# Expert weights from silu instead of exp, and a new order of the side steps

## The chip, the core and the metric

One core of a Trainium2 chip runs the whole kernel. Its engines are TensorE (PE in the profile, its weight loads PEld), VectorE (DVE), ScalarE (ACT), GpSimd (POOL) and SyncE (SP, which issues the DMAs). The metric is the time of one execution on the device, in microseconds; lower is better.

## The reference, cut to what matters

Four sequences of 1024 tokens with 128 features go through four residual blocks: a linear attention (a), a mixture of experts, a windowed softmax attention (b), and the same mixture of experts again. The change is in the routing of the experts:

```python
logits = x @ gate_w.T                                   # 32 experts
probs = jax.nn.softmax(logits.astype(jnp.float32), axis=-1)
top_w, top_idx = jax.lax.top_k(probs, TOP_K)            # the best 8
top_w = top_w / jnp.sum(top_w, axis=-1, keepdims=True)
comb = jnp.sum(jax.nn.one_hot(top_idx, NUM_EXPERTS, dtype=x.dtype) * top_w[..., None], axis=1)
...
y = u * jax.nn.silu(g) @ dw.T                           # for each expert, of every token
acc + y * w_e[:, None]
```

All 32 experts are computed for every token, and `comb` is zero for those that aren't among a token's best eight.

## The kernel before

**Tiling and stages.** A row is one sequence, with 8 tiles of 128 tokens. The unit of the expert work is a stage: half a row (four tiles, 512 tokens), first pass or second. `STREAM` lists the 16 stages in their order as (row, f), f being 0 and 1 for the two halves of the first pass and 2 and 3 for those of the second: stage 0 is (0, 0), stage 1 (0, 1), stage 2 (1, 0), stage 8 (2, 1). A stage has 16 chunks of two experts each. Of a chunk, PE computes gate and up (three products each, since weights and activations are split into a high and a low part; `gate_up`, lines 1519 to 1521), ACT takes the silu of the gate (line 1056), DVE multiplies it by up (`gated`, line 1304), POOL multiplies that by the experts' weights, spread over the partitions (`hidden`, line 872), and PE adds the chunk to the output (`down`, line 1542), three chunks later. Three pairs of PSUM banks hold gate and up, so PE runs at most three chunks ahead of ACT and DVE.

**Attention parts.** Between the stages stand parts of the windowed attention, in which no chunk runs: one of 8 tiles for each of the rows 0 to 2, and two of 4 tiles for row 3. A tile goes from PE (scores) to DVE (maxima), ACT (exp), DVE and POOL (normalising), PE (turning), DVE (copies) and PE (mixing).

**Side steps.** All other work is cut into named steps, such as the norms (x_stats, x_rstd, x_apply, x_turn; m_ and s_ for the other two norms), the linear attention (qkv, expo, elu, attend, kvsum, wterm, wred and the h_ steps), its MLP (attnT, mlp1, mlp2) and the routing. The order is written out by hand. `AHEAD` lists the steps that run before the first stage, together with the first six chunks of stage 0 (early n is gate and up of chunk n on PE, lead n its silu and its gated product). `PLAN` has for each stage or part a table from a slot to steps: in a stage, slot s stands behind chunk s on each engine; an attention part has three slots for each tile and three at its end, so 27 for 8 tiles. `own`, `ahead` and `back` say whether a step belongs to the row of the period, the next or the one before. Every engine walks the same list and does its share of each step, in that order, so a step that waits holds up all that stands behind it on its engine. PE's products of the side steps go through one PSUM bank, `side`, in the order of the list.

**The routing steps.** moe_turn, z_hi and z_lo bring the normalised tokens to the form that the products read; route and r_sum give `logits`, 128 tokens x 4 tiles x 32 experts. `top` (DVE) finds the eight largest of each tile, negates the first into `neg_top` and marks the eight in `replaced`. `weigh` (ACT, line 1012) takes exp(logits - maximum), one operation for each tile, since the bias differs. `comb` (DVE, lines 1286 to 1289) keeps the marked ones, sums them and inverts the sum; `cnorm` (ACT, line 1018) scales by it; `weighT` turns the result on PE (line 1461) and copies it (ACT, line 1025). Then SP (`send_weights`, `spread_quarter`) writes it to DRAM and reads it back, spread over 64 partitions for each expert: the first quarter of a stage in 8 DMAs, the others in two each, one buffer for the even quarters and one for the odd. POOL's `hidden` waits for its quarter. SP issues its DMAs in one order too: in the loop over the stages the loads of the next rows of x (`load_rows`) and quarters 2 and 3 of the stage, and then the weights of the next stage. The weights of stage 2 it sends at the end of row 0's attention part, ahead of the loads of row 2.

**Tables of ACT.** exp, gelu and silu each need a table of their own. The compiler puts a table load ahead of an operation whose function differs from the last of these three; copies, squares, relu and scaled copies need none. exp is used by the attention parts, by expo and by weigh, gelu by mlp1, silu by the chunks.

## Time and profile before

| what | value |
|---|---|
| timed runs | 966.5, 966.74 and 979.81 us; median 966.74 us |
| the profiled execution | 970.32 us, its span 968.5 us |
| mean granted clock of TensorE | 0.966 |
| busy share of the span | PE 92%, DVE 67%, ACT 63%, POOL 69% |

The span runs from the first to the last instruction; the execution's own time has 1.8 us around it. The busy share of PE counts matmuls whose ends are modelled, and it is an average over the whole span. The stages lie, by the start of each stage's first gate product, at 65 us (stage 0), 119.5 (stage 1), 217 (stage 2), 270, 311 and 355 (stages 3 to 5); the first attention part lies from 162 to 217 us, the second from 400 to 447.

### The profile page before, as it was taken

To read this page: it belongs to the slowest core of one execution; us is meant where nothing else is said; L and a number is where in the kernel's file an instruction comes from. 1 tells how busy PE (TensorE), PEld (TensorE's weight loads), DVE (VectorE), ACT (ScalarE), POOL (GpSimd) and SP (SyncE) were. 2 spreads that over 40 slices of the span, in tenths; PEclk is the share of its full clock that TensorE was granted. 3 is DMA by queue.
4 is the path that set the end of the run, shared out by engine and by line. 5 is a ranking of instruction groups with operands and counts; after the bars stand their busy time and mean duration, and the time that the engine had idled before them with its cause. 6 is when DMAs were issued, how large, how long until landed. Compare 5 with 4: busy or idle time off the path is not lost.

```text
span 968.5 us, 16816 instructions
## 1 busy us (share of the span) xinstructions
PE 895.2 (92%) x5456; PEld 623.2 (64%) x5456; DVE 653.0 (67%) x1471; ACT 611.6 (63%) x1876; POOL 663.8 (69%) x617
## 2 busy tenths in 40 slices
PE   2467999898999999999999999999999999999998
PEld 1145666685667666687666666687666667667665
DVE  5898876897768748698648756798635348447522
ACT  4446676993665576795775585896556377486531
POOL 6786888675687759576669768666666545646654
PEclk8559999999899999999999999999999999999999
DMA  6006254016343626240433534340344530713352
GB/s 193 0 1 142 52 128 89 2 46 136 64 123 76 139 60 157 58 121 13 98 92 87 146 83 108 74 129 17 87 106 102 135 68 27 159 38 102 88 133 65
DMA packets 64903, 85.75 MB, mean 89 GB/s; under 512 B 5232, under 2 KB 30768, under 8 KB 64560
## 3 DMA queue, kind: packets, MB, share of 16 engines
q1 hardware_dynamic: 64816, 84.68, 36.4%
q8 instruction: 43, 0.70, 0.3%
q14 instruction: 44, 0.36, 0.1%
HBM read 79.39 MB, written 5.28 MB: 87 GB/s over the span
## 4 chain that ended last, share of the span: by engine, by line
PE 69%; DVE 10%; ACT 7%; POOL 5%; issue 4%; DMA 3%; SPq 1%; DVEq 0%; ACTq 0%; POOLq 0%
PE bank L1542 19%; PE bank L1519 11%; PE bank L1521 10%; PE bank L1520 10%; ACT probs L1081 4%; PE bank L1578 4%; PE bank L1563 3%; PE bank L1592 2%; POOL work L872 2%; DVE probsT L1346 2%; PE bank L1406 1%; DMA spread_w<-comb_dram 1%; DVE w_terms L1188 1%; PE bank L1556 1%; DMA x_buf<-x 1%
## 5 line engine op out<-in xcount | busy, mean ns | idle before, releaser
L872 POOL TENSOR_TENSOR work<-work,spread_w 128x512 f32<-128x512 f32 x256 | 333.8, 1318 | 171.0 <-DVE work L1304 151.7
L1304 DVE TENSOR_TENSOR work<-work,bank 128x512 f32<-128x512 f32 x256 | 172.1, 683 | 185.3 <-PE bank L1521 93.1
L1542 PE MATMUL bank<-work,down_w 128*128 128x512 f32 x512 | 262.7, 598 | 1.9 <-POOL work L872 1.9
L1056 ACT ACTIVATE work<-bank 128x512 f32<-128x512 f32 x256 | 150.3, 596 | 176.5 <-PE bank L1521 171.9
L1519 PE MATMUL bank<-z_hi,gate_hi 128*128 128x512 f32 x256 | 168.0, 656 | 4.9 <-ACT work L1056 2.7
L1081 ACT ACTIVATE probs<-bank,neg_max 128x96 f32<-128x96 f32 x512 | 166.3, 386 | 5.5 <-DVE neg_max L1332 3.9
L880 POOL TENSOR_TENSOR probs<-probs,prob_inv 128x768 f32<-128x768 f32 x64 | 95.1, 1486 | 59.9 <-DVE prob_inv L1340 59.6
L1081 ACT ACTIVATION_READ_ACCUMULATOR probs<-bank,neg_max 128x1 f32 x512 | 127.6, 252 | 0.0
L1542 PEld LDWEIGHTS bank<-work,down_w 128*128 128x128 f32 x512 | 95.3, 189 | 29.6 <-POOL work L872 5.6
L1519 PE MATMUL bank<-z_hi,up_hi 128*128 128x512 f32 x256 | 101.8, 397 | 3.1 <-DVE work L1304 3.1
L1521 PE MATMUL bank<-z_hi,gate_lo 128*128 128x512 f32 x256 | 102.0, 398 | 0.0
L1521 PE MATMUL bank<-z_hi,up_lo 128*128 128x512 f32 x256 | 101.5, 397 | 0.0
L1520 PE MATMUL bank<-z_lo,gate_hi 128*128 128x512 f32 x256 | 101.2, 395 | 0.0
L1520 PE MATMUL bank<-z_lo,up_hi 128*128 128x512 f32 x256 | 100.4, 392 | 0.0
L829 POOL TENSOR_TENSOR kv_terms<-elu,qkv 128x1024 f32<-128x1024 f32 x32 | 81.8, 2562 | 12.5 <-DVE elu L1153 7.2
L1346 DVE COPY probsT<-bank 96x512 f32<-96x512 f32 x128 | 80.2, 666 | 3.6 <-PE bank L1578 3.2
L1332 DVE TENSOR_REDUCE neg_max<-bank 128x4 f32<-128x384 f32 x128 | 64.8, 547 | 20.1 <-PE bank L1563 19.2
L1519 PEld LDWEIGHTS bank<-z_hi,gate_hi 128*128 128x128 f32 x256 | 49.0, 191 | 42.4 <-issue 31.0
L1578 PE MATMUL bank<-ident,probs 128*96 128x128 f32 x512 | 69.8, 278 | 6.8 <-DVE probsT L1346 6.0
L1520 PEld LDWEIGHTS bank<-z_lo,gate_hi 128*128 128x128 f32 x256 | 49.3, 193 | 33.7 <-issue 30.6
L1563 PE MATMUL bank<-keysT,qm 32*128 32x96 f32 x1024 | 69.2, 269 | 0.0
L1563 PEld LDWEIGHTS bank<-keysT,qm 32*128 32x128 f32 x1024 | 66.4, 188 | 0.0
(155 smaller groups left out, 1467.2 us busy)
## 6 DMA issues: line engine op xcount, KB each, us to landing
spread_w<-comb_dram SPq DMA_DIRECT2D x96, 512.0 KB, 6.7
spread_w<-comb_dram SPq DMA_DIRECT2D x128, 128.0 KB, 3.0
vals<-v_dram SPq DMA_DIRECT2D x16, 384.0 KB, 4.0
x_buf<-x SPq DMA_DIRECT2D x8, 256.0 KB, 4.3
v_dram<-v_tok SPq DMA_DIRECT2D x8, 256.0 KB, 6.8
out<-xs SPq DMA_DIRECT2D x8, 256.0 KB, 3.1
spread_w<-wg SPq DMA_DIRECT2D x1, 1024.0 KB, 7.1
spread_w<-wu SPq DMA_DIRECT2D x1, 1024.0 KB, 9.2
```

Of the source, the lines that this page charges most:

```text
L872: pool.tensor_tensor(work[:, n % WORK], work[:, n % WORK], spread_w[:, n // EACH % 2, s % EACH], ALU.mult).then_inc(hid_gated, 1)
L880: pool.tensor_tensor(pr, pr, prob_inv[:, i % 2, part].unsqueeze(2).broadcast_to([P, HALF_BLOCKS, KW]), ALU.mult).then_inc(probs_normed, 1)
L1056: act.activation(work[:, n % WORK], bank[GATE_BANKS[ring_of(row, f, s)]], ACT.Silu).then_inc(silu_ready, 1)
L1081: a = act.activation(probs[:, i % 2, m], bank[hg][:, b * KW:(b + 1) * KW], ACT.Exp, bias=neg_max[:, i % 2, m:m + 1], accum_out=prob_sum[:, ...
L1304: dve.tensor_tensor(work[:, n % WORK], work[:, n % WORK], bank[UP_BANKS[ring_of(row, f, s)]], ALU.mult).then_inc(gated_ready, 1)
L1346: dve.tensor_copy(probsT[:, b], bank[4 + b % 2][0:KW, :]).then_inc(probsT_copied, 1)
L1519: pe.matmul(dst, w_hi[:, cols], h, start=True, stop=False)
L1520: pe.matmul(dst, w_hi[:, cols], l, start=False, stop=False)
L1521: pe.matmul(dst, w_lo[:, cols], h, start=False, stop=True).then_inc(ready, 1)
L1542: pe.matmul(bank[Y_BANK], down_w[:, c], work[:, n % WORK], start=(c == 0), stop=(c == CH - 1)).then_inc(down_done, 1)
L1563: mm = pe.matmul(bank[hg][:, KW * b:KW * (b + 1)], qm[feats, i // T, NB * (i % T) + b].rearrange("p j q -> p (j q)"), keysT[feats, first:f ...
L1578: mm = pe.transpose(bank[4 + b % 2][0:KW, P * hg:P * (hg + 1)], probs[:, i % 2, hg * NB + b], ident[:])
```

## The change

With m the maximum of a tile's logits and y = logit - m - 1, which is -1 or less, let s = silu(y) = y sigmoid(y). Then y - s = y (1 - sigmoid(y)), and s / (y - s) = sigmoid(y) / (1 - sigmoid(y)) = exp(y), which differs from the old value by a factor that the later division by the sum takes out. `top` now also subtracts m + 1 from the logits, in place, and signals only after that; `weigh` is one silu of all four tiles; `comb` gets a subtraction, a reciprocal and a multiplication more.

```diff
             def weigh(row, f):
                 act.wait_ge(top_ready, STAGE_AT[row, f] + 1)
-                for t in range(T):
-                    a = act.activation(expd[:, t], logits[:, t], ACT.Exp, bias=neg_top[:, t:t + 1])
-                a.then_inc(expd_ready, 1)
+                act.activation(expd[:], logits[:], ACT.Silu).then_inc(expd_ready, 1)
...
-                dve.tensor_scalar(neg_top[:], top[:, :, 0], -1.0, None, ALU.mult).then_inc(top_ready, 1)
+                dve.tensor_scalar(neg_top[:], top[:, :, 0], -1.0, -1.0, ALU.mult, ALU.add)
                 for t in range(T):
                     ins = dve.match_replace(replaced[:, t], top[:, t], logits[:, t], NEG)
                 step(ins)
+                dve.tensor_tensor(logits[:], logits[:], neg_top[:].unsqueeze(2).broadcast_to([P, T, NE]),
+                                  ALU.add).then_inc(top_ready, 1)
...
+                step(dve.tensor_tensor(logits[:], logits[:], expd[:], ALU.subtract))
+                step(dve.reciprocal(logits[:], logits[:]))
                 step(dve.scalar_tensor_tensor(out=comb[:], in0=replaced[:], scalar=TAKEN, in1=expd[:],
                                               op0=ALU.is_lt, op1=ALU.mult))
+                step(dve.tensor_tensor(comb[:], comb[:], logits[:], ALU.mult))
                 step(dve.tensor_reduce(top_sum[:], comb[:], AX_X, ALU.add))
```

The second part of the change is a new `PLAN` and a new `AHEAD`: the same steps in other slots, throughout. No step is added or dropped. Shown are the list ahead of the first stage, from its middle on, and the tables that the prediction speaks of; the other tables are as thoroughly changed.

```diff
 AHEAD = (
-    own(("masks", 0), ("x_stats", 0), ("x_rstd", 0), ("x_apply", 0), ("x_turn", 0), ("lam", 0),
-        ("qkv_first", 0), ("qkv_first", 1), ("qkv_first", 2), ("elu_first", 0), ("masks", 1), ("attend", 0),
-        ("x_stats", 1), ("elu_first", 1), ("qkv_first", 3), ("w_hi", 0), ("kvsum", 0), ("elu_first", 2),
...
-        ahead(("qkv_next", 0)) + own(("wred", 4), ("kvsum", 5), ("wterm", 5), ("wred", 5), ("kvsum", 6),
-        ("m_apply", 0), ("moe_turn", 0), ("w_lo", 1), ("z_hi", 0), ("z_lo", 0), ("wterm", 6), ("wred", 6)) +
-        ahead(("qkv_next", 1)) + own(("route", 0), ("r_sum", 0), ("attend", 7), ("early", 0), ("top", 0),
-        ("weigh", 0)) + ahead(("qkv_next", 2)) + own(("kvsum", 7), ("comb", 0), ("wterm", 7), ("masks", 2),
-        ("wred", 7), ("cnorm", 0), ("h_sq1", 1)) + ahead(("qkv_next", 3)) + own(("h_red1", 1), ("h_newton1", 1)) +
-        ahead(("expo", 0), ("elu", 0)) + own(("early", 1), ("early", 2), ("weighT", 0), ("lead", 0), ("lead", 1),
-        ("h_g2", 1)) + ahead(("attend", 0)) + own(("h_sq2", 1), ("early", 3), ("early", 4), ("early", 5)) +
-        ahead(("qscale", 0)) + own(("h_red2", 1), ("lead", 2)) + ahead(("attend", 1), ("kvsum", 0)) +
-        own(("lead", 3), ("lead", 4), ("lead", 5))
+    own(("masks", 0), ("x_stats", 0), ("x_rstd", 0), ("x_apply", 0), ("masks", 1), ("x_stats", 1),
+        ("x_rstd", 1), ("w_hi", 0), ("x_turn", 0), ("lam", 0), ("qkv_first", 0), ("qkv_first", 1), ("qkv_first", 2),
+        ("elu_first", 0), ("qkv_first", 3), ("attend", 0), ("elu_first", 1), ("attend", 1), ("elu_first", 2),
...
+        ahead(("x_apply", 0), ("x_turn", 0)) + own(("m_rstd", 0), ("m_apply", 0), ("attend", 7), ("wterm", 6)) +
+        ahead(("qkv_next", 0), ("qkv_next", 1)) + own(("wred", 6), ("moe_turn", 0), ("z_hi", 0), ("masks", 2),
+        ("z_lo", 0), ("route", 0)) + ahead(("qkv_next", 2)) + own(("kvsum", 7), ("wterm", 7), ("r_sum", 0),
+        ("wred", 7), ("h_sq1", 1), ("w_lo", 1), ("h_g2", 1)) + ahead(("qkv_next", 3), ("expo", 0)) +
+        own(("h_red1", 1), ("h_sq2", 1), ("top", 0), ("weigh", 0), ("h_newton1", 1), ("h_red2", 1), ("comb", 0),
+        ("cnorm", 0), ("h_pow2", 1), ("h_newton2", 1), ("early", 0), ("h_scale", 1)) + ahead(("elu", 0)) +
+        own(("early", 1), ("lead", 0), ("weighT", 0)) + ahead(("attend", 0)) + own(("lead", 1), ("early", 2),
+        ("h_gain", 1), ("h_sum", 1), ("lead", 2), ("lead", 3), ("early", 3)) + ahead(("qscale", 0), ("attend", 1),
+        ("kvsum", 0)) + own(("attnT", 1), ("x_add", 1), ("mlp1", 1)) + ahead(("wterm", 0)) + own(("early", 4),
+        ("mlp2", 1), ("lead", 4), ("lead", 5), ("early", 5), ("m_stats", 1))
 )
     (0, "attn"): {
-        0: ahead(("wred", 4), ("wterm", 5), ("z_hi", 0)),
+        0: ahead(("moe_turn", 0), ("z_hi", 0), ("kvsum", 5), ("wred", 4)),
...
-        11: own(("values", 1)) + ahead(("top", 0), ("weigh", 0)),
-        13: own(("bias", 1)),
-        15: ahead(("comb", 0), ("cnorm", 0)),
-        22: own(("proj", 0)),
-        23: own(("m_stats", 2), ("m_rstd", 2)),
-        25: ahead(("weighT", 0)),
+        8: ahead(("kvsum", 6)) + own(("queries", 1), ("queries_copy", 1)),
+        11: ahead(("route", 0), ("r_sum", 0), ("top", 0), ("weigh", 0)),
+        13: ahead(("wterm", 6)) + own(("values", 1)),
+        18: own(("bias", 0)) + ahead(("comb", 0), ("cnorm", 0)),
+        20: ahead(("weighT", 0)),
+        22: own(("bias", 1), ("proj", 0)),
+        26: ahead(("wred", 6)),
     },
     (1, "first"): {
-        0: back(("m_apply", 2)) + own(("kvsum", 6), ("wterm", 6)),
-        2: back(("proj", 1)) + own(("wred", 6), ("kvsum", 7)),
-        3: own(("wterm", 7)) + back(("moe_turn", 2)) + own(("wred", 7)) + ahead(("x_stats", 0)),
+        0: own(("kvsum", 7)),
+        2: back(("m_stats", 2), ("m_rstd", 2)),
+        3: own(("wterm", 7), ("wred", 7)) + back(("proj", 1)) + own(("h_sq1", 1), ("h_g2", 1)),
+        4: ahead(("x_stats", 0)) + own(("h_red1", 1)) + ahead(("x_rstd", 0)),
...
     (1, "attn"): {
-        0: ahead(("weighT", 0)),
+        2: ahead(("wterm", 7)),
...
     (2, "second"): {
-        15: own(("weighT", 1)),
     (2, "third"): {
+        0: ahead(("kvsum", 3), ("wterm", 3)) + own(("weighT", 1)),
...
     (2, "attn"): {
-        0: ahead(("weighT", 0), ("kvsum", 7)) + own(("bias", 1)),
-        2: ahead(("wterm", 7)) + back(("y_back", 3)),
+        0: ahead(("weighT", 0)),
+        2: back(("y_back", 3)),
```

The steps attnT 1, mlp1 1, mlp2 1 and m_stats 1 of row 0 stood in slots 6 and 7 of stage 0 and are now in `AHEAD`. weighT of the next stage stood in slot 14 of stages 0 and 2 and in slot 13 of stage 6, and now stands in slot 15 of them.

## Rows read from the trace of the kernel before

**Rows 1.** The page's first part: busy us, share of span, instructions.

```profile
PE 895.2 (92%) x5456; PEld 623.2 (64%) x5456; DVE 653.0 (67%) x1471; ACT 611.6 (63%) x1876; POOL 663.8 (69%) x617
```

**Rows 2.** The chain of waits by engine, in shares of the span.

```profile
PE 69%; DVE 10%; ACT 7%; POOL 5%; issue 4%; DMA 3%; SPq 1%; DVEq 0%; ACTq 0%; POOLq 0%
```

**Rows 3.** Timeline of PE, 929.8 to 940 us: start, duration, line, operation, tiles.

```profile
930.96 0.79 PE L1519 MATMUL bank<-z_hi,gate_hi 128*128 128x512 f32 x1
...
933.20 0.79 PE L1519 MATMUL bank<-z_hi,gate_hi 128*128 128x512 f32 x1
```

**Rows 4.** PE's waits, 270 to 400 us: total us, times, longest.

```profile
PE bank L1400 <- ACT zT L922: 0.5, 1, 0.5
```

**Rows 5.** Windows: length, busy us (instructions) by engine, PE clock, DMA share.

```profile
20.00:65.00 45.00, 19.61 (x46) 9.76 (x46) 40.97 (x62) 20.28 (x44) 36.45 (x30) 0.50 0.00 1
...
162.00:217.00 55.00, 51.91 (x629) 40.61 (x628) 46.03 (x112) 51.52 (x278) 36.45 (x33) 0.97 0.16 40
217.00:270.00 53.00, 48.26 (x245) 32.57 (x243) 39.75 (x87) 27.71 (x57) 31.93 (x34) 0.94 0.42 91
400.00:447.00 47.00, 45.06 (x623) 35.55 (x622) 39.12 (x83) 45.91 (x263) 32.70 (x30) 1.00 0.30 76
...
37.10:41.50 4.40, 1.65 (x2) 0.50 (x2) 4.02 (x13) 1.39 (x4) 2.96 (x5) 0.50 0.00 0
```

**Rows 6.** Groups by line, table loads: busy us, mean ns | idle before.

```profile
L1056 ACT ACT_TABLE_LOAD x32 | 41.1, 1283 | 1.3 <-ACT combT L1025 0.6 <-ACT v_tok L1048 0.2
...
L1012 ACT ACT_TABLE_LOAD x15 | 19.2, 1283 | 0.3
```

**Rows 7.** Timeline of ACT, 108 to 113 us.

```profile
111.08 1.28 ACT L1056 ACT_TABLE_LOAD   x1
112.38 0.60 ACT L1056 ACTIVATE work<-bank 128x512 f32<-128x512 f32 x1
```

**Rows 8.** Groups by line, DVE.

```profile
L1304 DVE TENSOR_TENSOR work<-work,bank 128x512 f32<-128x512 f32 x256 | 172.1, 683 | 185.3 <-PE bank L1521 93.1 <-ACT work L1056 87.3 <-issue 2.4
...
L1164 DVE TENSOR_REDUCE kv<-kv_terms 128x64 f32<-128x1024 f32 x32 | 38.9, 1214 | 7.9 <-POOL kv_terms L829 7.6
...
L1286 DVE SCALAR_TENSOR_TENSOR comb<-replaced,expd 128x128 f32<-128x128 f32 x16 | 6.7, 416 | 7.9 <-ACT expd L1012 7.3 <-DVE replaced L1278 0.4
...
L1232 DVE RECIPROCAL newton<-head_ms 128x64 f32<-128x64 f32 x8 | 4.4, 553 | 0.3
```

**Rows 9.** Timeline of DVE, in brackets the wait and what ended it.

```profile
13.90 0.43 DVE L1158 SCALAR_TENSOR_TENSOR elu<-elu,qkv 128x256 f32<-128x256 f32 x1 [2.66 <-ACT elu L950]
...
60.42 2.28 DVE L1176 TENSOR_TENSOR up_lo<-spread_w,up_hi 128x2048 fp32r<-128x2048 f32 x1
...
69.87 0.18 DVE L1289 RECIPROCAL top_inv<-top_sum 128x4 f32<-128x4 f32 x1
...
240.33 0.87 DVE L1139 BATCH_NORM_STATS2 stats<-x_buf 128x6 f32<-128x128 f32 x4 [4.50 <-DMA x_buf<-x]
```

**Rows 10.** Chain of waits, 73 to 95 us: start, us, what.

```profile
75.48 0.45 PE bank L1461 x4
```

**Rows 11.** Timeline of POOL, 40 to 125 us.

```profile
92.81 1.29 POOL L872 TENSOR_TENSOR work<-work,spread_w 128x512 f32<-128x512 f32 x1 [4.53 <-DMA spread_w<-comb_dram]
```

**Rows 12.** PE's waits, 65 to 120 us; last row 217 to 270.

```profile
PE bank L1406 <- ACT zT L922: 1.0, 1, 1.0
PE bank L1400 <- ACT z L931: 0.8, 1, 0.8
PE bank L1435 <- ACT attnT L922: 0.7, 1, 0.7
PE bank L1428 <- DVE attn L1240: 0.5, 1, 0.5
...
PE bank L1519 <- DVE work L1304: 3.1, 1, 3.1
```

**Rows 13.** The fused operation of comb: ns min/median/max, first and last start.

```profile
L1286 DVE SCALAR_TENSOR_TENSOR comb<-replaced,expd x16: 280/293/1015, 69.2 to 913.2; 128x128 f32<-128x128 f32 x16
```

More of the change, by code:

```diff
@@ L96 @@
-        11: ahead(("wred", 1)) + own(("route", 1), ("r_sum", 1), ("top", 1)) + ahead(("x_apply", 1)) +
-            own(("weigh", 1)) + ahead(("kvsum", 2)),
-        12: ahead(("x_turn", 1)) + own(("comb", 1)),
-        13: ahead(("qkv", 4), ("wterm", 2)) + own(("cnorm", 1)),
-        14: ahead(("wred", 2)) + own(("weighT", 1)) + ahead(("kvsum", 3), ("wterm", 3)),
-        15: ahead(("qkv", 5)),
+        0: ahead(("wred", 0)),
+        3: own(("m_rstd", 1), ("m_apply", 1)),
+        4: ahead(("x_stats", 1)),
@@ new lines @@
+        5: ahead(("x_rstd", 1)),
+        8: own(("moe_turn", 1), ("z_hi", 1)) + ahead(("kvsum", 1)) + own(("z_lo", 1)) + ahead(("wterm", 1),
+            ("attend", 2)),
+        9: own(("route", 1), ("r_sum", 1)),
+        10: ahead(("x_apply", 1)) + own(("top", 1)),
+        11: own(("weigh", 1), ("comb", 1)),
+        12: ahead(("x_turn", 1), ("wred", 1)),
+        13: ahead(("qkv", 4), ("kvsum", 2), ("wterm", 2), ("attend", 3)),
+        14: ahead(("wred", 2)) + own(("cnorm", 1)) + ahead(("qkv", 5), ("kvsum", 3), ("wterm", 3)),
@@ L149 @@
+        14: own(("h_scale", 1), ("h_gain", 1)) + back(("cnorm", 2)) + own(("h_sum", 1), ("x_add", 1)) +
+            ahead(("qkv", 3)),
+        15: back(("weighT", 2)),
     },
     (1, "second"): {
-        0: ahead(("kvsum", 0), ("qscale", 0), ("attend", 1)) + own(("attnT", 1)),
-        1: own(("mlp1", 1)),
-        2: own(("mlp2", 1), ("m_stats", 1), ("m_rstd", 1)) + ahead(("wterm", 0)),
-        4: ahead(("wred", 0)) + own(("m_apply", 1)),
-        5: ahead(("kvsum", 1), ("attend", 2)),
-        7: own(("moe_turn", 1), ("z_hi", 1)) + ahead(("wterm", 1)) + own(("z_lo", 1)),
@@ L157 @@
-        8: own(("route", 1)) + ahead(("wred", 1)) + own(("r_sum", 1), ("top", 1)),
-        11: ahead(("attend", 3)) + own(("y_back", 0), ("s_stats", 0), ("weigh", 1), ("s_rstd", 0)) +
-            ahead(("kvsum", 2)) + own(("comb", 1)) + ahead(("wterm", 2)),
-        12: ahead(("wred", 2)),
-        13: own(("cnorm", 1), ("s_apply", 0)),
-        14: own(("weighT", 1)),
-        15: ahead(("kvsum", 3)) + own(("seq_turn", 0)) + ahead(("x_stats", 1)),
+        0: ahead(("expo", 0)) + own(("attnT", 1)),
@@ new lines @@
+        2: ahead(("elu", 0), ("attend", 0)) + own(("mlp1", 1)),
+        3: own(("mlp2", 1), ("m_stats", 1)) + ahead(("kvsum", 0)) + own(("m_rstd", 1)),
+        5: ahead(("qscale", 0)) + own(("y_back", 0), ("s_stats", 0), ("m_apply", 1)),
+        6: ahead(("wterm", 0)) + own(("moe_turn", 1), ("z_hi", 1)) + ahead(("wred", 0), ("attend", 1)),
+        7: ahead(("x_stats", 1)),
+        8: own(("z_lo", 1)) + ahead(("kvsum", 1)),
+        9: own(("route", 1), ("r_sum", 1), ("top", 1), ("weigh", 1), ("comb", 1), ("s_rstd", 0)) +
+            ahead(("x_rstd", 1)),
@@ L189 @@
[L189 to L196 removed]
+        1: ahead(("mlp2", 0), ("m_stats", 0)),
@@ L239 @@
+        8: ahead(("attend", 2)),
+        9: own(("weigh", 1)) + ahead(("x_rstd", 1)) + own(("s_apply", 0)) + ahead(("wred", 0)) +
+            back(("m_stats", 3)),
+        11: ahead(("kvsum", 1)),
+        12: ahead(("wterm", 1)) + own(("seq_turn", 0)),
+        13: ahead(("wred", 1), ("x_apply", 1)) + own(("comb", 1)) + ahead(("kvsum", 2)),
+        14: ahead(("wterm", 2), ("attend", 3), ("wred", 2), ("x_turn", 1)),
+        15: back(("m_rstd", 3)) + own(("keys", 0), ("cnorm", 1)),
     },
@@ L290 @@
+        5: own(("h_pow2", 1), ("h_newton2", 1), ("h_scale", 1)) + back(("m_apply", 2), ("proj", 1)),
+        7: back(("moe_turn", 2)) + own(("h_gain", 1), ("h_sum", 1), ("x_add", 1)),
+        8: back(("z_hi", 2), ("z_lo", 2)),
+        9: back(("route", 2), ("r_sum", 2), ("top", 2)),
+        10: own(("attnT", 1)) + back(("weigh", 2)),
+        11: back(("comb", 2), ("cnorm", 2)),
+        13: back(("weighT", 2)),
     },
```

349 lines of the change are left out of this document (164 added, 185 removed).

## The prediction

> **What bounds the kernel now.** I read the page first: TensorE (PE) is busy 895.2 of 968.5 us [rows 1]. The chain of waits says the same: 69% of the span is PE, 10% VectorE (DVE), 7% ScalarE (ACT) [rows 2]. Since a busy PE can hide small gaps, I then looked at a stretch with no side steps: the first product of a chunk starts at 930.96 and the next chunk's at 933.20, so a chunk takes 2.24 us [rows 3], and 256 chunks need 573 us however the other engines do. From 270 to 400 us, a stretch of three expert stages full of side steps, PE waited for another engine 0.5 us in all [rows 4]. There a cheaper ACT or a dearer DVE step changes nothing. What is left are three places, which the windows show [rows 5]: the lead-in (20 to 65 us: PE 19.61 of 45, DVE 40.97, so DVE bounds, at half clock), the first attention part (162 to 217: PE 51.91, ACT 51.52, DVE 46.03 of 55, all three near full) and the stage after it (217 to 270: PE 48.26 of 53 at a mean clock of 0.94). A later attention part (400 to 447) has PE 45.06, ACT 45.91 and DVE 39.12 of 47. The change is judged by these.
>
> **ACT: what the formula takes away.** Each exp inside an expert stage costs a table load before it, and one before the next silu. The trace has 15 loads at the exp line and 32 at the silu line [rows 6], 1.283 us each. Walking ACT's program order in the source, counting a load at each change of function among exp, gelu and silu, gives 66 loads before (those two lines agree) and 40 after: 26 fewer, 26 x 1.283 = 33.4 us of ACT. Nearly all is hidden: the chain of waits shows ACT's silu loads only twice, once behind a weigh, at 111.08 [rows 7], once behind a gelu, which stays. So on the path it is worth 1.3 us, and I count that below with the stage where it lies. The load at 111.08 is followed by the silu at 112.38, so a switch costs its 1.283 us and nothing more [rows 7]. The Trainium skill (ScalarE: Activation LUTs, "What ACT_TABLE_LOAD costs") adds a drain to every switch and gives about 2.66 us in all; by it ACT would be freed of 26 x 2.66 = 69 us rather than 33, but as an estimate for the path it would still be one switch. The first attention part goes the other way: its weigh is now silu among exps, so it gets two loads, +2.6 us, where ACT has 3.5 us free [rows 5].
>
> **DVE: what it adds.** Per weigh an add, a subtraction and a multiplication of 128x128 and a 128x128 reciprocal. No such reciprocal is in the trace. The step comb's fused operation of the same shape has two operands from SBUF, as the new ones have, and averages 0.416 us [rows 8]. Reciprocals: 0.553 us for 64 columns [rows 8] and 0.18 for 4 [rows 9]; the line through both gives 0.95 us for 128 columns, which I take because both ends are this kernel's; the bounds are 0.553 and twice that, 1.11. Sum 3 x 0.416 + 0.95 = 2.2 us a weigh (1.8 to 2.4), 35 us in all, and weights that come later by that and by the match_replace that top_ready now follows. In the expert stages the cover is DVE's idle time ahead of the gated product, 185.3 us over 256 chunks or 11.6 a stage [rows 8]; if it were gone, 2.2 us a stage would reach PE two chunks later. Uncovered are the weighs of the lead-in and of the first attention part.
>
> **The lead-in and stage 0.** The new order puts x_stats 1 and w_hi 0 into DVE's 2.66 us wait at 13.9 us [rows 9]; I take 2.2 us gained (0 to 2.66). z_lo now follows w_lo 1 at 62.7 [rows 9]; in the new list two steps of the linear attention of about the same length stand there instead, so z_lo comes at 60.5. From there to the end of comb, at 70.05 now [rows 9], the new list has three such steps as before, and besides w_lo 1 (2.28 us) [rows 9], h_red1, h_newton1 and h_red2 of the second half (for the first half the stretch from 37.1 to 41.5, with 4.02 us of DVE) [rows 5] and the new formula (2.2). So comb ends 8.5 - 2.2 = 6.3 us later, at 76.35, and with about 1 us for cnorm the transposition of the weights can run at 77.4. Now it runs at 75.48 [rows 10], since it stood behind a gate product that waited. So the weights leave 1.9 us later. POOL's fifth hidden product, at 92.81 now [rows 11], comes 17.3 us behind that transposition because its quarter of the weights comes last: +1.9. Against it, attnT 1, mlp1 1, mlp2 1 and their waits (0.5 and 0.7 us) leave stage 0 for the time in which POOL waits anyway, and two more PE waits of stage 0 go, 1.0 us for zT behind the weigh's table load and 0.8 us for z [rows 12]: -3.0. Net -1.1 us; bounds -4.8 (the weights not later, half a chunk gained) and +5 (PE, waiting with a lower clock, loses the 1.9 us twice, and none of the waits goes).
>
> **First attention part and the stage after.** Into attention 0 go kvsum 5 and 6, wterm 6 and wred 6, about 1.2 us each [rows 8], 4.8 us; m_stats 2 leaves it, 1.3 us (0.87 for the statistics, as in [rows 9], the rest an estimate for their aggregation); the formula adds 2.2: 5.7 us of DVE. DVE is busy 84% of this part, so I take 84%, +5 us (0 if all falls into its idle time, +8.3 with ACT's two loads on top). After it, the first expert stage of row 1 loses time for one reason that I can see. SP sends the weights of that stage and only then loads the next rows of x; DVE's x_stats waits 4.50 us for them, until 240.33 [rows 9], with the gated products queued behind it, and PE waits 3.1 us for those [rows 12]; the clock of 0.94 over 53 us is another 3.2 us [rows 5]. The new order transposes these weights in slot 20 of 27 instead of 25; at 55/27 us a slot that is 10 us earlier, SP is past them 10 us earlier, and the rows are there in time. I take -6 (0 to -6.3).
>
> **The rest.** Attention 1 gets wterm 7 (+1.2), attention 2 loses kvsum 7 and wterm 7 (-2.4): at 83% busy -1 (-2.4 to +1.2). weighT of stage 8 moves from the last slot of the stage before into slot 0 of its own; 17.3 us from transposition to the fifth product stand against seven chunks of 2.24 us, 15.7, and what side steps lie between them: +1 (0 to +3). Other PE steps only change places in stages where PE has no gap: 0 (-2.6 to +2).
>
> **Sum.** -1.1 + 5 - 6 - 1 + 1 = -2.1 us. The profiled execution took 970.32 us, its span 968.5 and 1.8 around it; it stands 3.6 above the median of the three timed runs, 966.74. So 968.2 in a profiled execution, and 966.7 - 2.1 = **964.6 us** timed.
>
> **Rivals.** (a) *Weights too late*, ending on the slower side: the formula lengthens the path from logits to weights by 2.2 us and more, and four transpositions move to slot 15 or 0. For: POOL's 4.53 us wait at 92.81 [rows 11]. Against: from slot 15 eight chunks, 18 us at least, are left for the 17.3. It decides when a quarter lands after its chunk's down product is due; each such stage then loses about 3.1 us of waiting and 3.2 of clock as in [rows 5, 12]. One such stage and the upper price of attention 0: 964.6 + 6.3 + 3.3 = 974; four stages: 990. (b) *The new order gains more*: the lead-in's idle PE is the only large reserve, 25 us of the 45 [rows 5]. If DVE's list there is 4.8 us better and attention 0 costs nothing, 964.6 - 3.7 - 5 = 956; below 947 it would need 10 us more of that lead-in, for which DVE has only 4 us of idle time in that window. (c) *DVE and POOL block each other*: comb's fused operation takes 0.280 us at best and 1.015 at worst [rows 13], so it sometimes stands still while POOL works. If the three new ones always took 1.015, a weigh costs 1.8 us more: 29 us, of which the lead-in and attention 0 show 3.6, and POOL's products as much: 964.6 + 7 = 972. The Trainium skill (SBUF — State Buffer, "SBUF: two separate sides") has this as a rule: a DVE operation with two SBUF inputs and a GpSimd operation exclude each other for the whole instruction. It speaks against this change, which adds 48 such operations; the mean of 0.416 shows it to strike rarely. (d) *The loads don't vanish*, if the silu of the weigh were given a table of its own: ACT as before, and the order alone remains, 966.
>
> **How the numbers follow.** Forecast 0.54, (a) 0.19 (of it 0.05 four stages late), (b) 0.17 (of it 0.08 below 947), (c) 0.08, (d) 0.02. Two per cent, 19 us, is about what a measurement of this kernel can tell from no change, since the three runs spread by 13 us. So faster 0.08, the same 0.87, slower 0.05. The range of 8 in 10 takes in (c), most of (a) and the nearer half of (b), and the bounds of lead-in and attention 0: 953 to 977.
>
> **What the profile would show.** 40 table loads, none at the weigh line but two, ACT some 40 us less busy, DVE some 35 more. Reciprocals of 0.95 us. The weights' first transposition at 77 and stage 0 ending at 118.4 instead of 119.5. A first attention part of 60 us, DVE over 85% busy in it, and no DVE wait for x in the stage behind. PE without waits in the later expert stages. The prediction is wrong if the lead-in moves by more than 5 us, or if PE waits for POOL in expert stages.

## The result, and the profile after

The changed kernel takes 980.64 us (median of four, 978.22 to 985.28) against 966.91 for the kernel before beside it: a ratio of 1.0124, with a 95% interval of 1.0093 to 1.0155. It is slower, by less than 2%, where I had forecast 2 us faster; the time lies above my range. The profiled execution took 979.21 us, span 977.5, so 8.9 us over that of before. A ratio leaves out executions more than 1.5% above the fastest of their kernel; in run e4 below these are three of ten, the profiled one (978.95 us) among them.

What the change does to the engines came out as worked out. First part of the page after, to be read beside [rows 1]:

```profile
PE 903.9 (92%) x5456; PEld 628.7 (64%) x5456; DVE 686.3 (70%) x1535; ACT 566.2 (58%) x1802; POOL 671.8 (69%) x617
```

Groups by line of the changed kernel: table loads at the silu and at the weigh line, then the formula's new operations (busy us, mean ns), beside [rows 6, 8].

```profile
L1057 ACT ACT_TABLE_LOAD x17 | 21.8, 1283 | 0.3
...
L1014 ACT ACT_TABLE_LOAD x2 | 2.6, 1283 | 0.0
...
L1290 DVE RECIPROCAL logits<-logits 128x128 f32<-128x128 f32 x16 | 15.2, 953 | 0.6
...
L1281 DVE TENSOR_TENSOR logits<-logits,neg_top 128x128 f32<-128x128 f32 x16 | 7.2, 453 | 0.5
L1293 DVE TENSOR_TENSOR comb<-comb,logits 128x128 f32<-128x128 f32 x16 | 5.8, 360 | 0.5
L1289 DVE TENSOR_TENSOR logits<-logits,expd 128x128 f32<-128x128 f32 x16 | 5.6, 347 | 1.9 <-ACT expd L1014 1.9
```

ACT is 45.4 us less busy, of which 33.4 are the 26 loads; DVE 33.3 more. Neither can be read off the total, since PE is busy 903.9 of the 977.5 us. So the time must be looked for by stretch. I took the start of each stage's first gate product (line 1519 before, 1525 after) in both traces; my terms of the sum stand beside the differences:

| stretch | before, us | after, us | difference | forecast |
|---|---|---|---|---|
| lead-in and stage 0 | 119.5 | 118.3 | -1.2 | -1.1 |
| stage 1 with attention 0 | 97.4 | 101.8 | +4.4 | +5 |
| stage 2 | 52.9 | 46.2 | -6.7 | -6 |
| stages 3 and 4 | 85.1 | 84.8 | -0.3 | 0 |
| stage 5 with attention 1 | 89.8 | 100.0 | +10.2 | +1 |
| stages 6 to 9 with attention 2 | 220.9 | 223.1 | +2.2 | -1 |
| rest | 303.0 | 303.3 | +0.3 | 0 |

One row is off by ten. Windows of the changed kernel (busy us, then the granted clock, DMA share, GB/s), beside [rows 5]:

```profile
162.00:220.00 58.00, 52.11 (x629) 40.17 (x628) 50.73 (x119) 53.44 (x273) 38.78 (x36) 0.97 0.17 38
220.00:266.00 46.00, 44.08 (x239) 30.08 (x238) 37.62 (x88) 22.10 (x54) 30.54 (x33) 1.00 0.44 104
400.00:427.00 27.00, 26.13 (x366) 20.69 (x365) 24.64 (x51) 26.30 (x156) 18.29 (x16) 1.00 0.35 92
424.00:434.00 10.00, 8.91 (x91) 7.27 (x91) 7.21 (x16) 6.33 (x38) 7.16 (x7) 0.68 0.57 129
434.00:444.00 10.00, 10.00 (x90) 8.34 (x88) 5.79 (x12) 5.52 (x34) 4.29 (x5) 0.50 0.00 0
```

In the second attention the granted clock is 1.00 (2.4 GHz) until 427 us and then 0.50 (1.2 GHz); the clock's own records put the fall at 427.64, inside PE's wait shown next, and the return 23.9 us later, where the part ends. Before, it was 1.00 throughout [rows 5]. From 434 to 444 PE is busy 10.00 of 10 us: at the low level PE sets the pace alone, and nothing can be caught up. PE's timeline shows what went before (its first row, from the lead-in, is taken up further below):

```profile
76.80 1.04 PE L1467 MATMUL bank<-ident,comb 128*32 128x128 f32 x4 [4.01 <-ACT comb L1019]
...
423.43 1.08 PE L1584 MATMUL bank<-ident,probs 128*96 128x128 f32 x8
...
425.75 1.08 PE L1598 MATMUL bank<-probsT,vals 96*32 96x128 f32 x32
427.92 1.94 PE L1584 MATMUL bank<-ident,probs 128*96 128x128 f32 x8 [1.09 <-POOL probs L883]
```

The same eight turnings take 1.08 us and then 1.94. Between them PE waited 1.09 us for POOL's normalising. POOL's timeline there:

```profile
422.39 1.27 POOL L860 TENSOR_TENSOR x_buf<-x_buf,bout_all 128x512 f32<-128x512 f32 x1
423.62 1.47 POOL L883 TENSOR_TENSOR probs<-probs,prob_inv 128x768 f32<-128x768 f32 x1
425.17 1.27 POOL L842 TENSOR_TENSOR attn<-attn,g_row 128x512 f32<-128x512 f32 x1
426.41 1.46 POOL L883 TENSOR_TENSOR probs<-probs,prob_inv 128x768 f32<-128x768 f32 x1
```

Two side steps of 1.27 us, bias (line 860) and h_g2 (842), stand ahead of two normalisings in a row (883). The new order has bias 1 in slot 11 and h_sq1 1, h_g2 1 in slot 12; the old one had bias and h_sq1 in slot 9 and h_g2 in 13. In the kernel before, two normalisings (at 424.17 and 426.82) lie between the same two steps (lines 857 and 839 there), and from 395 to 450 us PE never waits for POOL:

```profile
422.81 1.27 POOL L857 TENSOR_TENSOR x_buf<-x_buf,bout_all 128x512 f32<-128x512 f32 x1
...
428.25 1.27 POOL L839 TENSOR_TENSOR attn<-attn,g_row 128x512 f32<-128x512 f32 x1
```

### The profile page after: what moved, and what is told of

Same layout as the page of the kernel before. It is cut to its first block and busy times, and to the rows that moved or that the text cites. A ratio compares the mean times of both kernels' runs of the same rounds, so it can differ in the third digit from the quotient of the medians.

```text
span 977.5 us, 16807 instructions
## 1 busy us (share of the span) xinstructions
PE 903.9 (92%) x5456; PEld 628.7 (64%) x5456; DVE 686.3 (70%) x1535; ACT 566.2 (58%) x1802; POOL 671.8 (69%) x617
## 5 line engine op out<-in xcount | busy, mean ns | idle before, releaser
L875 POOL TENSOR_TENSOR work<-work,spread_w 128x512 f32<-128x512 f32 x256 | 340.2, 1345 | 149.4 <-DVE work L1310 135.5
L1082 ACT ACTIVATE probs<-bank,neg_max 128x96 f32<-128x96 f32 x512 | 165.9, 382 | 14.6 <-DVE neg_max L1338 13.3
L1526 PE MATMUL bank<-z_lo,up_hi 128*128 128x512 f32 x256 | 100.2, 392 | 0.0
L1584 PE MATMUL bank<-ident,probs 128*96 128x128 f32 x512 | 75.5, 293 | 9.6 <-DVE probsT L1352 5.8
L1525 PEld LDWEIGHTS bank<-z_hi,gate_hi 128*128 128x128 f32 x256 | 48.9, 191 | 40.9 <-issue 33.3
L1584 PEld LDWEIGHTS bank<-ident,probs 128*96 128x96 f32 x512 | 57.4, 134 | 23.2 <-issue 11.7
L1569 PE MATMUL bank<-keysT,qm 32*128 32x96 f32 x1024 | 71.8, 277 | 0.0
```

The lines of the kernel that those rows point to most:

```text
L875: pool.tensor_tensor(work[:, n % WORK], work[:, n % WORK], spread_w[:, n // EACH % 2, s % EACH], ALU.mult).then_inc(hid_gated, 1)
L1082: a = act.activation(probs[:, i % 2, m], bank[hg][:, b * KW:(b + 1) * KW], ACT.Exp, bias=neg_max[:, i % 2, m:m + 1], accum_out=prob_sum[:, ...
L1525: pe.matmul(dst, w_hi[:, cols], h, start=True, stop=False)
L1526: pe.matmul(dst, w_hi[:, cols], l, start=False, stop=False)
L1569: mm = pe.matmul(bank[hg][:, KW * b:KW * (b + 1)], qm[feats, i // T, NB * (i % T) + b].rearrange("p j q -> p (j q)"), keysT[feats, first:f ...
L1584: mm = pe.transpose(bank[4 + b % 2][0:KW, P * hg:P * (hg + 1)], probs[:, i % 2, hg * NB + b], ident[:])
```

## The experiments

My main theory (A): that crowding makes the wait, the wait brings the lower clock, and that costs the ten microseconds. Rivals: the formula itself (B, later split into its table loads, T, and its DVE work, D), another moved step (C), values that come late in attention 0 (V). Each ratio is against runs of the kernel before on the same chip (their medians 966.91 to 970.28 us). The two columns on the right are the stretches of the table above, from the profiled execution.

| run | median us | ratio (95%) | stage 1 + attention 0 | stage 5 + attention 1 |
|---|---|---|---|---|
| e1_formula | 985.18 | 1.0193 (1.0137 to 1.0249) | 112.7 | 91.7 |
| e2_order | 978.77 | 1.0093 (1.0062 to 1.0123) | 107.0 | 90.4 |
| e3_split | 974.59 | 1.0065 (1.0037 to 1.0092) | 103.1 | 89.2 |
| e4_crowd | 972.65 | 1.0019 (0.9989 to 1.0048) | 96.3 | 100.5 |
| e5_tables | 987.18 | 1.0171 (1.0128 to 1.0213) | 107.8 | 91.8 |
| e6_hybrid | 978.65 | 1.0111 (1.0054 to 1.0168) | 96.5 | 91.6 |
| e7_spread | 977.65 | 1.0077 (1.0052 to 1.0102) | 112.0 | 89.2 |
| e8_mend | 978.61 | 1.0077 (1.0038 to 1.0115) | 103.4 | 89.2 |
| e9_values | 984.48 | 1.0127 (1.0071 to 1.0183) | 108.5 | 89.2 |
| e10_best | 980.74 | 1.0101 (1.0060 to 1.0141) | 110.6 | 91.3 |
| e11_cut | 973.60 | 1.0055 (1.0019 to 1.0090) | 97.4 | 89.7 |
| e12_again | 982.52 | 1.0103 (1.0051 to 1.0155) | 103.9 | 100.0 |
| e13_early | 978.07 | 1.0079 (1.0044 to 1.0115) | 107.4 | 89.2 |
| e14_both | 972.34 | 1.0034 (1.0004 to 1.0063) | 100.2 | 97.6 |
| e16_red | 971.22 | 1.0028 (0.9992 to 1.0063) | 99.8 | 89.3 |
| e15_mix | 970.75 | 1.0012 (0.9974 to 1.0050) | 106.4 | 93.4 |
| e17_turn20 | 963.06 | 0.9952 (0.9921 to 0.9983) | 101.6 | 91.2 |
| e18_turn17 | 963.44 | 0.9955 (0.9933 to 0.9977) | 97.0 | 89.7 |

**The crowd in slots 11 and 12.** e3 moves one step out of it in the changed kernel, e4 puts the crowd into the kernel before, e12 is the changed kernel again.

```diff
 e3, (1, "attn") of the changed kernel
-        12: ahead(("h_sq1", 1), ("h_g2", 1)),
+        12: ahead(("h_sq1", 1)),
+        16: ahead(("h_g2", 1)),
 e4, (1, "attn") of the kernel before
-        9: ahead(("wred", 7)) + own(("bias", 1)) + ahead(("h_sq1", 1)),
-        13: ahead(("h_g2", 1)),
+        9: ahead(("wred", 7)),
+        11: own(("bias", 1)),
+        12: ahead(("h_sq1", 1), ("h_g2", 1)),
```

> The changed kernel with one step moved: the gain of row 1's second half (a POOL multiplication of 1.27 us) goes from slot 12 of the second attention to slot 16. A: TensorE no longer waits 1.09 us for the normalising at 427, the granted clock stays at 1.0 from 400 to 450 us, the second attention's last-chunk gap falls from 58.1 to 47 to 49 us, and the time is 968 to 971 us. B and C: the fall stays, 977 to 983 us.

> The kernel before with three steps put where the changed kernel has them: bias of row 1 in slot 11 of the second attention, square and gain of the next half in slot 12. A: a wait of TensorE for POOL's normalising of 0.8 us or more there, the clock falls to 0.5, and the time rises by 6 to 11 us to 973 to 978 us. If the attention of the kernel before, in which VectorE is late and POOL has time in hand, takes the two POOL steps without a wait, no change (966 to 968 us): then the crowding counts only together with something else of the change. B and C: 966 to 968 us.

> The changed kernel itself once more. Theory A: the fall of the clock near 427 us recurs with the same wait of 1.1 us for POOL, stage and second attention 99 to 101 us together, time 978 to 985 us. If the fall was that one execution's chance: 89 to 91 us in this profile, and times from 968 us on.

Windows of e3 and then of e4, 430 to 452 us, PE's wait in e4, and two of PE's waits in e12, the first of them for later:

```profile
430.00:452.00 22.00, 19.66 (x278) 15.90 (x275) 20.04 (x44) 18.19 (x98) 16.82 (x18) 1.00 0.23 51
```

```profile
430.00:452.00 22.00, 21.91 (x179) 18.11 (x180) 12.37 (x24) 14.32 (x80) 10.59 (x11) 0.50 0.07 19
```

```profile
429.91 1.94 PE L1579 MATMUL bank<-ident,probs 128*96 128x128 f32 x8 [1.14 <-POOL probs L881]
```

```profile
212.85 1.76 PE L1598 MATMUL bank<-probsT,vals 96*32 96x128 f32 x32 [2.66 <-DMA vals<-v_dram]
...
431.83 1.94 PE L1584 MATMUL bank<-ident,probs 128*96 128x128 f32 x8 [1.09 <-POOL probs L883]
```

With h_g2 four slots later the wait and the fall are gone, and the stretch is 89.2 us instead of 100.0; with the crowd the kernel before gets both, and 100.5 instead of 89.8. In e12 all recurs, down to the 23.9 us. A holds in the profiled executions of these runs. In the times it is worth less: e3's ratio is 1.0065 where the changed kernel has 1.0124 and 1.0103, an estimate of 4 to 6 us for the crowd, and e3 missed its 968 to 971 us; it lies 6 us above the kernel before. Of e4's ten executions six took 970 to 973 us, one 962.68 and three 979 to 987; the median, 972.65, is 4 us above the kernel before and just short of the 973 to 978 expected. So, to judge by the times, the crowd doesn't bring the fall each time.

**Formula and order by themselves.** e1 has the old order and the new weights, e2 the new order and the old weights.

> The new weights from silu with the order of steps of the kernel before. Theory A (the three steps bias, square and gain that stand together in slots 11 and 12 of the second attention keep POOL from the normalising; TensorE waits 1.09 us for it, its granted clock falls from 1.0 to 0.5 and stays there for 24 us, which costs about 10 us): this kernel does not have them together, so no fall of the clock between 390 and 460 us, and 963 to 968 us, ratio to the kernel before 0.996 to 1.001. Theory B (the formula costs the time: four more VectorE instructions for each weighing and weights that come later): 972 to 982 us, the second attention longer than 50 us. Theory C (another of the moved steps): as A here.

> The new order of steps with the old weights (four exponentials for each weighing). A: the three steps stand together as in the changed kernel, so the clock falls to 0.5 in the second attention and the time is 975 to 985 us. B: without the formula the loss goes, 958 to 966 us. C: as A in time, 975 to 985 us.

e1 overturned my view that the formula costs nothing: it is the slowest of all, and its loss lies in attention 0, 112.7 against 97.4. In e2 PE waits just as in the changed kernel, yet the clock stays at 1.00 in this execution:

```profile
435.10 1.08 PE L1581 MATMUL bank<-ident,probs 128*96 128x128 f32 x8 [1.10 <-POOL probs L883]
```

So a wait of 1.1 us can come with the fall and need not. What else decides is open. e2's loss in the profile is in attention 0 too, where its clock was low for 17 us from 204; that its time lies in A's range of 975 to 985 us is luck.

**What the formula does in attention 0.** Its weighing of stage 2 lies there. On e1, e5 takes the table loads away and keeps DVE's work; e6 takes both.

```diff
 e5 and e6, weigh
-                act.activation(expd[:], logits[:], ACT.Silu).then_inc(expd_ready, 1)
+                how = ACT.Exp if (row, f) == (1, 0) else ACT.Silu
+                act.activation(expd[:], logits[:], how).then_inc(expd_ready, 1)
 e6, comb
+                formula = (row, f) != (1, 0)
+                if formula:
+                    step(dve.tensor_tensor(logits[:], logits[:], expd[:], ALU.subtract))
+                    step(dve.reciprocal(logits[:], logits[:]))
...
+                if formula:
+                    step(dve.tensor_tensor(comb[:], comb[:], logits[:], ALU.mult))
```

> The old order with the new weights, but the one weighing that lies inside the first attention (row 1, first quarter) applies exp instead of silu, so the table of the attention's own exponentials stays loaded; VectorE's formula for it is still done, its last product into a buffer that nobody reads. Theory T (the formula alone cost 17 us because this weighing puts two table loads, 2 x 1.28 us, between the exponentials of an attention; TensorE waits and its granted clock falls there for up to 27 us): the first attention takes 97 to 101 us with its stage instead of 112.7, time 968 to 974 us. Theory D (VectorE's four more instructions, 2.2 us, are what delays the attention): no change, 982 to 987 us.

> As the run before, and VectorE's three further operations of the formula for that weighing (subtract, reciprocal, product: 1.5 us) are left out too. T: within 2 us of the run before, 967 to 973 us. D: the whole loss goes only here, 967 to 971 us against 982 to 987 us in the run before.

Timeline of DVE in e5, then PE's wait for the copy at its end:

```profile
206.56 0.37 DVE L1287 TENSOR_TENSOR logits<-logits,expd 128x128 f32<-128x128 f32 x1
206.97 0.95 DVE L1288 RECIPROCAL logits<-logits 128x128 f32<-128x128 f32 x1
...
208.93 0.18 DVE L1294 RECIPROCAL top_inv<-top_sum 128x4 f32<-128x4 f32 x1
209.03 0.19 DVE L1345 RECIPROCAL prob_inv<-prob_sum 128x8 f32<-128x8 f32 x1
209.13 1.26 DVE L1351 COPY probsT<-bank 96x512 f32<-96x512 f32 x2
```

```profile
209.94 1.91 PE L1583 MATMUL bank<-ident,probs 128*96 128x128 f32 x8 [1.55 <-DVE probsT L1351]
```

The comb step stands in one piece, 206.56 to 209.1, ahead of the copy of probsT; PE waits 1.55 us, and the clock falls for 20 us. Windows of e5 and of e6, 209 to 230 us:

```profile
209.00:230.00 21.00, 20.06 (x163) 17.23 (x164) 13.55 (x28) 13.23 (x73) 9.62 (x9) 0.52 0.01 2
```

```profile
209.00:230.00 21.00, 19.69 (x249) 15.39 (x250) 18.87 (x40) 15.16 (x71) 14.63 (x20) 1.00 0.08 25
```

With the table loads out and DVE's work kept, nothing is won (987 against 985 us); with DVE's three operations out as well, 8.5 us are gained, and the stretch is 96.5. There were four executions of each, and one of e6's took 989.32, so the 8.5 are rough. So D is enough for the loss in the old order, but T isn't cleared by it. ACT's timeline of e1, then PE's:

```profile
202.62 1.28 ACT L1011 ACT_TABLE_LOAD   x1
...
204.24 1.28 ACT L1079 ACT_TABLE_LOAD   x1
```

```profile
206.99 0.33 PE L1559 MATMUL bank<-window,same_query 32*128 32x384 bf16 x1 [0.39 <-ACT probs L1079]
208.28 0.34 PE L1559 MATMUL bank<-window,same_query 32*128 32x384 bf16 x1 [0.96 <-ACT probs L1079]
```

In e1 PE waits for exponentials that stand behind the two loads, the clock falls at 208.48 and stays low for 27.3 us, and DVE's subtraction starts only at 211.13. So there the fall follows T's waits, and in e5, without them, D's. Taking D out alone, with the loads left in, was not tried. e6 still lies 1.1% above the kernel before, in small pieces: stage 0 and the stretches with attention 1 and from stage 6 are each 1.8 to 2.5 us longer.

**Late values, and mends.** In the changed kernel PE waits for the values that go through DRAM, 1.28 us in the first profile and 2.66 in e12 (at 212.85 in its timeline above). The new order has them in slot 13, the old one in 11. e9 puts them back into 11 but ahead of the router's product; e13 puts that into slot 10; e14 is e13 with the edit of e6. All three have e3's split.

```diff
 (0, "attn"), e9
-        11: ahead(("route", 0), ("r_sum", 0), ("top", 0), ("weigh", 0)),
-        13: ahead(("wterm", 6)) + own(("values", 1)),
+        11: own(("values", 1)) + ahead(("route", 0), ("r_sum", 0)),
+        13: ahead(("wterm", 6), ("top", 0), ("weigh", 0)),
 (0, "attn"), e13 and e14, instead
+        10: ahead(("route", 0), ("r_sum", 0)),
+        11: own(("values", 1)) + ahead(("top", 0), ("weigh", 0)),
+        13: ahead(("wterm", 6)),
```

> The changed kernel with the gain in slot 16 of the second attention and, in the first attention, the values of row 0's second half in slot 11 (as in the kernel before) instead of slot 13, the top and weigh steps behind them in slot 13. Theory V (the first attention loses because the values go to DRAM and come back two slots later: TensorE waits 1.3 to 2.9 us for that load near 210 us and the clock falls behind it): the wait for vals goes, the first attention with its stage takes 98 to 101 us instead of 101.8 to 103.1, time 970 to 973 us. Theory T/D (table loads and the formula's VectorE work in this attention): the wait for vals goes but the stage stays at 101 to 108 us, 973 to 977 us.

> The changed kernel with the gain in slot 16 of the second attention, and in the first attention the router's product in slot 10 and the values in slot 11, both as in the kernel before (top and weigh stay in slot 11, silu). V (late values are the loss of the first attention): no wait for vals, the stage with this attention takes 98 to 101 us instead of 101.8 to 103.9, time 970 to 973 us. T/D (table loads and VectorE's formula): the wait for vals goes, but a wait for the exponentials or for VectorE's copy of 1 us or more stays near the weighing; 101 to 108 us, 973 to 978 us.

> As the run before, with exp and no formula for the weighing inside the first attention. V: as the run before, within 1 us. T/D: 2 to 5 us less than it; the stage with the first attention takes 96 to 99 us and the time is 967 to 971 us.

e9 took one wait away and put another there: the router's product waits until ACT has emptied the side bank of the values (PE's timeline of e9), and the clock falls behind it.

```profile
195.31 0.30 PE L1458 MATMUL bank<-router_hl,z_hi 128*128 128x64 f32 x1 [2.59 <-ACTq L1052]
```

In e13 the wait for the values is gone, but the stretch still takes 107.4 us, with 1.9 us of waits for ACT's exponentials and 2.0 for DVE's copies: V alone is not the loss. e14 gains 5.7 us on e13 in the median (972.34 against 978.07, 11 executions each) and 7 in the stretch: T and D together cost that here; which of them wasn't tried in this order. In e14's profile the second attention falls to the low level without any crowd, behind another wait:

```profile
434.29 1.93 PE L1604 MATMUL bank<-probsT,vals 96*32 96x128 f32 x32 [1.93 <-DMA vals<-v_dram]
```

e7 deals out four steps of one slot in stage 6 on top of e3, e8 adds the edit of e6 to that:

```diff
 e7, (2, "first") and (2, "second")
-        13: own(("mlp1", 1), ("mlp2", 1), ("m_stats", 1), ("m_rstd", 1)),
+        13: own(("mlp1", 1)),
...
-        15: ahead(("expo", 0), ("elu", 0), ("attend", 0)) + back(("weighT", 2)) + own(("m_apply", 1)),
+        15: own(("mlp2", 1)) + ahead(("expo", 0), ("elu", 0), ("attend", 0)) + back(("weighT", 2)) + own(("m_stats", 1), ("m_rstd", 1)),
...
+        0: ahead(("qscale", 0)) + own(("m_apply", 1)),
```

> The changed kernel with the gain moved to slot 16 of the second attention, as before, and the four steps that share slot 13 of row 2's first stage (two MLP products, statistics, inverse deviation) dealt over slots 13, 15 and slot 0 of the next stage. If TensorE's wait for the gelu between the two products is what makes that stage longer (its slot takes 5.14 us, others 2.7 to 2.9 us), the stage falls from 50 to 47 to 48 us and the time by 2 us, from 974.6 to 972 to 973 us; if the stage's length has another reason, 974 to 976 us.

> The changed kernel with all three mends: gain in slot 16, the slot of four steps dealt out, exp and no formula for the weighing inside the first attention. A and T together: no fall of the clock in the second attention, the first attention 98 to 101 us with its stage instead of 101.8 to 103.1, time 965 to 971 us. If the rest of the new order costs what is left of the loss: 972 to 975 us.

Both missed: stage 6 stayed at 50.4 and 50.6 us, so the crowded slot was not its loss, and attention 0 varied from one profile to the next (e7's clock averaged 0.59 from 180 to 217 us in its profile; e3, equal up to there, had one short fall in this part).

e16 moves DVE's small steps in attention 1 forward on top of e14; e15 joins the mends with the old order from row 2 on; e10 was a first try at that, with e9's fault in it; e11 has the old order up to row 1 and the new one after, with the old weights.

```diff
 e16 and e15, (1, "attn")
-        23: ahead(("h_red1", 1), ("h_newton1", 1)),
-        24: ahead(("h_sq2", 1)),
+        18: ahead(("h_red1", 1), ("h_sq2", 1)),
+        26: ahead(("h_newton1", 1)),
 e15 and e10: PLAN from (2, "first") on is that of the kernel before, and
+FORMULA = {(0, 0), (0, 1), (0, 2), (0, 3), (1, 1), (2, 0)}
...
+                how = ACT.Silu if (row, f) in FORMULA else ACT.Exp
 e11: PLAN from (2, "first") on is that of the changed kernel, the rest is the kernel before
```

> A mixture: the new order for the lead-in and the rows 0 and 1, with the gain in slot 16 and the values in slot 11, the order of the kernel before from row 2 on; weights from silu where the weighing lies in an expert stage of that first part, from one exp everywhere else (no formula there, so none inside the first attention). If the causes are the clock's fall in the second attention, the first attention's table loads, VectorE work and late values, and the stages of row 2: 961 to 966 us, ratio 0.991 to 0.998. If the new order costs in a way that is not yet named: 968 to 973 us.

> The kernel before (old weights) up to the end of row 1, the new order from row 2 on. If the later stages of the new order cost what the trace shows (stages 6 and 7 longer by 2 to 5 us, the last attentions shorter by 1 to 2 us): 1 to 4 us over the kernel before, 969 to 972 us. If they cost nothing, within 1 us of it.

> As the run before, and in the second attention the mean square of the halves and the second square go from slots 23 and 24 to slot 18, the Newton step to slot 26. If VectorE's row of eight small operations in the last slots (446.8 to 449.4 us in the run with the gain moved) is what TensorE waits 1.7 us for: 1 to 2 us less than the run before, 966 to 969 us, and the first stage of row 2 falls from 50 to 48 to 49 us. If not, the same time.

> All mends together with the order of the kernel before from row 2 on and one exp for every weighing there. If the named causes are all of the loss: 960 to 966 us, faster than the kernel before by 3 to 9 us. If the new order has a cost in the first two rows that is not named: 967 to 973 us.

e16's longest wait in that place is 0.8 us instead of e3's 1.7, and its median is 1.1 us under e14's, which these runs can't tell from nothing; the expected 966 to 969 us were missed. e11 shows that the late stages of the new order cost something whatever the weights: 223.4 us for stages 6 to 9 against 220.9, and 973.60 us in the median, somewhat over the 969 to 972 expected. e10 is slow as e9 is: the router's product waits 2.59 us again. e15 takes 965.5 to 978 us: with every named cause out, the kernel is as fast as before, not faster, and its median of 970.75 lies in the range expected for a cost not yet named. In its profile attention 0 still falls, though T, D and V are out: after PE's waits of 0.56 and 0.17 us for DVE's copies (202.55 and 203.14) the clock is low for 17 us from 203.65. e16 runs the same steps up to there and has the same two waits (203.12 and 203.72), yet its clock stays high, and its stretch takes 99.8 us instead of 106.4. So one profile's length of attention 0 is no measure of an edit to within 7 us; the medians must carry the comparison.

**Where the gain came from.** The new order gains 6.7 us in stage 2. The prediction put that down to weighT of stage 2, turned earlier; that step alone is moved in the kernel before, to slot 20 (e17) and 17 (e18).

```diff
 (0, "attn") of the kernel before
+        20: ahead(("weighT", 0)),
         22: own(("proj", 0)),
         23: own(("m_stats", 2), ("m_rstd", 2)),
-        25: ahead(("weighT", 0)),
```

> The kernel before with one step moved: weighT of stage 2 from slot 25 of the first attention to slot 20, as in the changed kernel. If the early turning is the gain (the next rows of x come in time, VectorE no longer waits 4.5 us for them, TensorE not 3.1 us for VectorE): stage 2 falls from 52.9 to 46 to 48 us, the attention stays at 55 us, time 961 to 965 us, ratio 0.992 to 0.996. If the gain is that work left stage 2 for the attention: stage 2 stays at 52 to 53 us and the time within 1 us of the kernel before.

> The same with the turning in slot 17, three slots earlier still. Early turning: as the run before or up to 1 us less, 960 to 965 us, unless TensorE now waits for the weights in the attention (a wait for comb of 1 us or more there, and the clock falls: 972 to 980 us). Work left: as the kernel before.

Timeline of DVE in e18: the statistics of the next x, which waited 4.50 us before [rows 9], and its windows for stage 2 and for the time from stage 0 to attention 0:

```profile
235.62 0.86 DVE L1139 BATCH_NORM_STATS2 stats<-x_buf 128x6 f32<-128x128 f32 x4
```

```profile
217.00:262.00 45.00, 43.43 (x237) 29.91 (x237) 36.64 (x87) 27.01 (x57) 32.76 (x34) 1.00 0.39 87
...
85.00:215.00 130.00, 122.61 (x914) 86.14 (x915) 101.27 (x234) 99.88 (x359) 98.81 (x89) 1.00 0.35 81
```

The wait is gone, stage 2 takes 45.3 us (45.4 in e17) instead of 52.9, and with one step moved, no formula and no new order, the kernel beats both: 963.06 and 963.44 us. From 71 us on e18's clock records show no fall until 958 us. In e17's profile attention 0 is longer than was expected (101.6 us for the stretch); its clock was low there for 10 us from 191.7, ahead of the moved step, which runs at 215.34.

## Why the prediction was wrong

**Right.** The loads (40, two at the weigh line), the reciprocal (0.953 us against 0.95), the lead-in with stage 0 (-1.2 against -1.1), and the stage behind the first attention (-6.7 against -6) with its cause, which e17 and e18 show. weighT of stage 8 in the new slot cost nothing (42.3 us against 42.4), where +1 was forecast. weighT in the lead-in was due at 77.4 and ran at 76.80 (the first row of PE's timeline above). The 4.01 us that PE waits for it there I hadn't named; the lead-in with stage 0 came out as long as forecast all the same. POOL's quarter that came 4.53 us late [rows 11] now comes 1.17 late.

**The step that failed** is the one under "The rest": attentions 1 and 2 together -1, from DVE's mean share of 83%. Attention 1 alone cost +10.2 in the profile. A mean share says how much fits into the part, not whether two steps of one queue fit between two tiles. I had costed the steps that came in or went out and left out those that only changed places, and POOL's queue with them; and I had charged a wait with the low clock in stage 2, from [rows 5], but gave it no price in the attentions, where PE is busy 45 of 47 us and where a wait can end in the same way. This step is not all of the miss: in e3's profile, without the fall, the kernel is still 4.1 us longer than before, with +1.8 in the lead-in and stage 0, +5.7 in stage 1 with attention 0 and +3.7 in stages 6 to 9 against -6.7 in stage 2.

**Right by luck, then mis-sized: the first attention.** +5 was 84% of DVE's added work, and the first profile has +4.4. But PE's waits for DVE's copies there, 0.9 us in all, are those of before; what rose most are its waits for ACT's exponentials, from 0.3 to 1.4 us, and for the values, from nothing to 1.28, neither of them a term of the +5 (ACT's loads stood in the bound alone). Other profiled executions of this order with the formula gave +5.7, +6.5 and +14.6 (e3, e12, e7). There my bound of +8.3 was too low for the same reason, the clock. e14 against e13 sizes the formula in it, loads and DVE's work together, at 5.7 us; in the old order e6 against e5 sizes DVE's three operations at a rough 8.5. The forecast's two bounds for the lead-in are not what its terms give: -3.0 and half a chunk of 2.24 us make -4.1 and not -4.8, and 1.9 lost twice makes 3.8 and not 5; neither bound came into play.

**Rivals.** (a) named weights that come too late; PE's longest wait for POOL's hidden product, in stage 0, is 1.0 us, and no stage shows that price. (c) is out: the three new two-input operations average 0.347 to 0.453 us, beside 0.416 for comb's before, and POOL's hidden product went from 1318 to 1345 ns. The Trainium skill (SBUF — State Buffer, "SBUF: two separate sides") says that such pairs exclude each other; the few operations that last longer than their usual 0.29 agree with it (the longest, 1.372 us at 745.65, runs beside a POOL addition of 1.28 us), and the sum of 2.1 us a weigh shows that it costs little here. (b) had a part of the truth, a gain that the kernel before had left; it came with one step and not with the order. (d) is out by the count.

**Open.** Why e2's wait of 1.10 us left the clock alone, and e16's shorter ones, where e15's did not; what lengthens stages 6 and 7 by 2.1 and 1.4 us (e11 ties it to the order, e7 rules out one slot); and how often attention 0 of the changed kernel falls, since each profile shows one execution.

## What to carry to other kernels

Where the pacing engine is busy almost throughout a part (here 45 of 47 us), deal the side steps out by engine and by tile, for every engine's queue, and count those that only change places: two of 1.27 us in adjacent slots of POOL cost 10 us here in the executions in which the clock fell behind them. Read the granted clock by windows before blaming a formula or an order, since a wait of about 1 us came back tenfold, and look at more than one execution. Take a broad change apart: one step of it, moved alone, was worth 6 us, and all else in it was worth less than nothing.

## What the runs showed of the hardware

A wait of TensorE of 1.09 to 1.14 us in a part where it was otherwise busy came with a fall to 1.2 GHz that lasted 23.9 us, alike in three executions of two kernels (427.64 us in the changed kernel, 429.82 in e4, 431.55 in e12), while PE was busy all the time (10.00 of 10 us) at that level; a wait of 1.10 us in a fourth execution left it at 2.4 GHz. After waits of 0.56 and 0.17 us the clock fell for 17 us in e15 and stayed in e16. So the length of the last wait alone doesn't tell whether the clock falls. Taking two table loads of 1.283 us out from between the exponentials gained nothing in the old order as long as DVE's three operations stayed (e5 against e1).
